# Layer 3 of a four-layer cross-attention kernel: the softmax probabilities transposed by VectorE and DMA in place of TensorE, with the work orders of layers 2 and 3 rewritten

## The reference, cut to what matters

```python
q = (hidden_state @ Wq + bq).reshape(b, l, KVH, GROUPS, HD).transpose(0, 2, 3, 1, 4)
k = (encoder_hidden_state @ Wk + bk).reshape(b, s, KVH, HD).transpose(0, 2, 1, 3)
v = (encoder_hidden_state @ Wv + bv).reshape(b, s, KVH, HD).transpose(0, 2, 1, 3)
scores = jnp.einsum('bkgld,bksd->bkgls', q, k) * scale + mask
attn = jax.nn.softmax(scores, axis=-1)
out = jnp.einsum('bkgls,bksd->bkgld', attn, v)          # needs the probabilities with s on partitions
x = out.transpose(0, 3, 1, 2, 4).reshape(b, l, H) @ Wo + bo + hidden_state
# layer norm of x, times gamma, plus beta
```

## Time and profile before

| what | value |
|---|---|
| median of three runs | 2391.65 us |
| the profiled execution itself | 2392.45 us |
| its span in the profile | 2390.7 us |
| TensorE matmul busy | 2244.4 us (94%) |
| VectorE, ScalarE, GpSimd busy | 1078.3, 1087.6, 580.0 us |
| mean granted clock of TensorE | 0.975 of full speed |

### The profile page before, as it was taken

How to read it: one execution, slowest core, us unless ns; L and a number is a source line. 1 busy time by engine, 2 the same in 40 slices (tenths; PEclk the granted TensorE clock), 3 DMA queues, 4 the chain that set the end, 5 groups by cost and what they waited for, 6 DMA issues and landing times. The chain is left out here.

```text
span 2390.7 us, 57498 instructions
## 1 busy us (share of the span) xinstructions
PE 2244.4 (94%) x22784; PEld 1637.0 (68%) x22784; DVE 1078.3 (45%) x3052; ACT 1087.6 (45%) x3441; POOL 580.0 (24%) x605
## 2 busy tenths in 40 slices
PE   7886999999999999999957999999999999999986
PEld 3444776676777777766546777777777777777754
DVE  4662322222222222222144565566665555666642
ACT  4553333333333333333223465566655655666554
POOL 0000100000000000000034444434444443344420
PEclk9997999999999999999978999999999999999998
DMA  4532000000000000000141001111010111110100
GB/s 163 171 105 64 16 19 19 19 19 19 19 19 19 19 19 19 19 10 5 76 133 21 16 21 26 22 26 22 21 26 16 26 26 22 26 21 16 21 20 10
DMA packets 116698, 81.94 MB, mean 34 GB/s; under 512 B 79136, under 2 KB 91808, under 8 KB 114208
## 3 DMA queue, kind: packets, MB, share of 16 engines
q1 hardware_dynamic: 106240, 48.35, 8.0%
...
...
## 5 line engine op out<-in xcount | busy, mean ns | idle before, releaser
L751 PEld LDWEIGHTS bank<-normedT,mlp_w 128*128 128x128 f32 x2048 | 235.0, 193 | 18.1 <-issue 17.1
L751 PE MATMUL bank<-normedT,mlp_w 128*128 128x128 f32 x2048 | 241.0, 278 | 0.8 <-DVE normedT L981 0.8
L761 PE MATMUL bank<-mlp_w,geluT 128*128 128x512 f32 x512 | 228.9, 596 | 0.0
L932 DVE CUSTOM_DVE_ANT_0 probs<-quad,neg_mask 128x256 f32<-128x256 f32 x256 | 90.8, 420 | 275.1 <-PE quad L681 275.1
L1975 ACT ACTIVATE scores<-scores,nmax 128x128 f32<-128x128 f32 x512 | 198.3, 396 | 2.5 <-DVE nmax L2237 2.5
L1463 POOL TENSOR_TENSOR k_even_odd<-k_even_odd,decay_products 128x512 f32<-128x512 f32 x80 | 98.1, 1227 | 328.1 <-PE quad L1659 251.6
L939 DVE COPY probsT<-quad 128x512 f32<-128x512 f32 x128 | 84.8, 683 | 191.6 <-PE quad L695 191.2
L761 PEld LDWEIGHTS bank<-mlp_w,geluT 128*128 128x128 f32 x512 | 93.8, 190 | 103.3 <-issue 103.3
L867 ACT ACTIVATE geluT<-bank,cols 128x128 f32<-128x128 f32 x256 | 73.0, 368 | 177.3 <-PE bank L751 177.3
L1391 POOL TENSOR_TENSOR gn_rstd<-gn_var_eps,halfs 128x32 f32<-128x32 f32 x16 | 87.0, 5435 | 170.2 <-DVE gn_var_eps L2160 170.2
L875 ACT ACTIVATE probs<-probs,nmax 128x256 f32<-128x256 f32 x256 | 126.1, 494 | 2.0 <-DVE nmax L932 1.8
...
## 6 DMA issues: line engine op xcount, KB each, us to landing
x_in<-in_x SPq DMA_DIRECT2D x32, 256.0 KB, 2.9
...
ctx_in<-in_ctx SPq DMA_DIRECT2D x16, 256.0 KB, 2.9
l_out<-wy ACTq DMA_DIRECT2D x16, 256.0 KB, 2.3
wy_in<-l_out SPq DMA_DIRECT2D x16, 256.0 KB, 3.5
hT<-in_ctxT SPq DMA_DIRECT2D x16, 256.0 KB, 3.5
l_out<-l_x ACTq DMA_DIRECT2D x16, 256.0 KB, 2.1
x_in<-l_out SPq DMA_DIRECT2D x16, 256.0 KB, 2.5
```

Source lines behind the costliest of these rows:

```text
L751: mm = nc.tensor.matmul(PS[b][:, f * P:(f + 1) * P], mlp_w1[:, c, m * P:(m + 1) * P], nT[:, c, :], start=(c == 0), stop=(c == NC - 1))
L761: mm = nc.tensor.matmul(PS[M.bank][:, :], gT[:, f, :], mlp_w2[:, f, :], start=(f == 0), stop=(f == NF - 1))
L932: mx = nc.vector.tensor_tensor_reduce(probs[:, h, :], PS[b][:, e * 256:(e + 1) * 256], negm[:, :], -1.0 / D1, 3.0e38, ALU.add, ALU.min, nm ...
```

## The change

The probabilities of all eight units now lie in one tile, `sc`, of nine rows of 512 numbers per partition. Row 0 is spare. The units of a half share four rows: unit k writes, for each of its four blocks of 128 columns, four runs of 32 numbers, one into each row of its half (`prob`). So a row holds 32-token blocks of every unit of its half. `a_turn` is now one VectorE instruction, which transposes each 32x32 block of row k+1 within its 32 partitions and writes row k. It can only start when the exponentials of the whole half are made. `a_move`, new on SyncE's queue, then moves four blocks of 32 partitions each to their place in `scT` with four transfers of 64 KB. `scT` is one tile for both halves, so `a_move` 4 to 7 wait until `a_value 0` is done. `a_value`, `a_norm` and `a_max` follow the new layout; VectorE's `a_norm` is two instructions. `v` now lies in the tile `z`, and `n_shift`, which writes `z`, waits for the spread of `v`. The PSUM copies of `a_turn` on ScalarE are gone. The banks and all five orders are new.

```diff
-        v = sb("v2", [P, NC, HC, D2])
+        v = z[:, :, :].rearrange("p c (h j) -> p c h j", h=HC)
...
-        sc = [sb(f"scores{u}", [P, 2, 2, P]) for u in range(NU)]
-        scT = [sb(f"probsT3_{q}", [P, 2, 2, P]) for q in range(RG)]
+        sc = sb("scores3_turned", [P, 2 * RG + 1, D])
+        scT = sb("probsT3", [P, 2, RG, D // 2])
...
         ORDER = dict(
-            pe=[("p_t5",), ("a_x",), ("w_var",), ("p_t5t",), ("b_out",), ("p_mix",), ("a_q",), ("a_kv",), ("p_mix4",), ("p_k",),
-                ("w_rstd",), ("a_score", 0), ("p_u1",), ("p_r",), ("a_score", 1), ("p_w",), ("w_out",), ("a_turn", 0), ("p_level",
-                0), ("p_g",), ("a_turn", 2), ("p_level", 1), ("w_xc",), ("p_v",), ("a_turn", 3), ("p_level", 2), ("a_turn", 1),
-                ("n_xa",), ("w_fr",), ("p_level", 3), ("w_fk",), ("p_level", 4), ("a_turn", 4), ("a_value", 0), ("a_turn", 7),
-                ("a_turn", 5), ("p_level", 5), ("a_turn", 6), ("w_fv",), ("p_level", 6), ("a_norm",), ("a_value", 1), ("p_s0",),
+            pe=[("p_t5",), ("a_kv",), ("p_t5t",), ("w_var",), ("a_x",), ("p_mix",), ("b_out",), ("a_q",), ("p_mix4",), ("p_k",),
+                ("w_rstd",), ("a_score", 0), ("p_u1",), ("p_r",), ("a_score", 1), ("p_w",), ("w_out",), ("p_level", 0), ("p_v",),
+                ("p_level", 1), ("w_xc",), ("p_g",), ("p_level", 2), ("w_fk",), ("p_level", 3), ("a_value", 0), ("n_xa",),
+                ("p_level", 4), ("w_fr",), ("p_level", 5), ("w_fv",), ("p_level", 6), ("a_norm",), ("p_s0",), ("a_value", 1),
                 ("p_av",), ("p_av6",)],
...
+            act=[("p_t5",), ("p_t5t",), ("a_kv",), ("a_x",), ("p_xm", 0), ("p_xm", 2), ("p_xm", 3), ("p_xm", 1), ("p_xm", 4),
+                 ("a_q",), ("p_k",), ("b_store",), ("p_u1",), ("w_rstd",), ("a_exp", 0), ("p_r",), ("p_w",), ("a_exp", 2), ("a_exp",
+                 3), ("a_exp", 1), ("a_exp", 7), ("a_exp", 6), ("p_v",), ("a_exp", 5), ("w_xc",), ("a_exp", 4), ("p_g",), ("w_fk",),
+                 ("n_xa",), ("w_fr",), ("a_norm",), ("p_level6",), ("a_bias",), ("p_wkv",)],
+            dve=[("n_ln1",), ("w_var",), ("p_xm", 0), ("p_xm", 2), ("n_nx",), ("b_out",), ("p_xm", 1), ("p_xm", 3), ("b_ln",),
+                 ("w_rstd",), ("a_max", 1), ("a_max", 0), ("a_max", 2), ("a_max", 3), ("p_xm", 4), ("w_gate",), ("a_max", 6),
+                 ("a_max", 5), ("a_max", 7), ("a_max", 4), ("p_rup", 0), ("w_out",), ("p_merge", 0), ("a_turn", 0), ("a_turn", 1),
+                 ("w_ln2",), ("a_turn", 2), ("p_merge", 1), ("a_turn", 3), ("p_rup", 1), ("w_sx",), ("w_xk",), ("p_s0c",), ("p_rup",
+                 2), ("p_merge", 2), ("w_xr",), ("a_turn", 4), ("a_rinv",), ("a_turn", 5), ("p_rup", 3), ("p_merge", 3), ("a_turn",
+                 6), ("p_gate",), ("a_turn", 7), ("p_rup", 4), ("p_merge", 4), ("p_merge", 5), ("p_rup", 5), ("n_shift",), ("p_rup",
+                 6), ("w_fv",), ("a_norm",)],
+            pool=[("n_rstd",), ("w_pow",), ("p_xm", 0), ("b_rstd",), ("p_xm", 2), ("w_first",), ("w_rep",), ("p_xm", 1), ("p_xm",
+                  3), ("p_k0",), ("p_ur",), ("p_wl",), ("w_rstd2",), ("p_kup", 0), ("p_xm", 4), ("p_kup", 1), ("p_kup", 2),
+                  ("p_kup", 3), ("p_kup", 4), ("p_s0b",), ("n_first",), ("a_x3b",), ("p_kup", 5), ("a_norm",)],
+            sp=[("a_move", 0), ("a_move", 1), ("p_v",), ("a_move", 2), ("a_move", 3), ("w_lda",), ("a_move", 4), ("a_move", 5),
+                ("a_move", 6), ("a_move", 7), ("n_ldx",), ("n_lds0",), ("p_ldw",)])
...
+        def prob(k, c, e):
+            at = 256 * e + 64 * (k % RG) + SB * c
+            return sc[:, RG * (k // RG) + 1:RG * (k // RG) + 1 + RG, at:at + SB]
...
+                def a_move(i, uses, k):
+                    half, m = k // RG, k % RG
+                    if half or later(i):
+                        sp.wait_ge(s_av, 2 * i + half)
+                    sp.wait_ge(s_turned, NU * i + k + 1)
+                    for q in range(RG):
+                        sp.dma_start(scT[SB * m:SB * m + SB, :, q, :],
+                                     sc[SB * q:SB * q + SB, k, :].rearrange("p (e n) -> p e n", e=2)).then_inc(s_moved, 16)
...
-                def a_turn(i, uses, k):
-                    pe.wait_ge(s_exp, NU * i + rank("act", "a_exp", k) + 1)
-                    turn4(uses[("a_turn", k)], BANK["a_turn", k], sc[k][:, :, :, :].rearrange("p a e q -> p (a e q)"))
...
-                    for t in latest([uses[("a_turn", RG * half + r)] for r in range(RG)]):
-                        pe.wait_ge(t.free, t.done)
+                    pe.wait_ge(s_moved, 16 * RG * (NU * i + RG * half + RG))
                     for e in range(2):
                         for r in range(RG):
                             mm = nc.tensor.matmul(PS[OAV][SB * r:SB * r + SB, half * 256:(half + 1) * 256], v3[:, r, e, :],
-                                                  scT[r][:, :, e, :], start=(e == 0), stop=(e == 1))
+                                                  scT[:, e, :, 64 * r:64 * r + 64], start=(e == 0), stop=(e == 1))
...
-                    nc.scalar.activation(scT[k % RG][:, :, :, :].rearrange("p a e q -> p (a e) q"),
-                                         chunked(PS[BANK["a_turn", k]][:, :]), ACT.Copy).then_inc(u.free, 1)
...
                 def a_norm(i, uses):
                     u, ps = use(uses, "a_norm")
+                    act.wait_ge(s_moved, 16 * RG * (NU * i + RG))
...
+                    if later(i):
+                        dve.wait_ge(s_v2, 64 * i)
                     nc.vector.tensor_tensor(sx[:, :, :], xaT[:, :, 0:P], xaT[:, :, 1:P + 1], ALU.subtract)\
...
+                def a_turn(i, uses, k):
+                    half = k // RG
+                    dve.wait_ge(s_exp, NU * i + 1 + max(rank("act", "a_exp", q) for q in range(RG * half, RG * half + RG)))
+                    if k == 0 and later(i):
+                        dve.wait_ge(s_attnT, i)
+                    elif k:
+                        dve.wait_ge(s_turned, NU * i + k)
+                    dve.sem_inc(s_hold, 1)
+                    nc.vector.transpose(sc[:, k, :], sc[:, k + 1, :]).then_inc(s_turned, 1)
```

More of the change, by code:

```diff
@@ L1157, in layers23 @@
         rinv = sb("rinv3", [P, KV3, G3])
[L1158 to L1160 removed]
+        attn = sc[:, 0, :].rearrange("p (c q) -> p c q", c=NC)
+        rrep, y, out = sc[:, 8, :], sc[:, 5, :], sc[:, 6, :]
         attnT = sb("attnT3", [P, NC, P])
@@ L1231, in layers23 @@
         S = {k: (sem(f"l23_{k}_psum_ready"), sem(f"l23_{k}_psum_free")) for k in ("quad", 5, 6, 7)}
-        USES = {("n_xa",): (7, 1), ("p_t5",): (6, 1), ("p_t5t",): (6, 1), ("p_mix",): ("quad", RG), ("p_mix4",): ("quad", 1),
-                ("p_u1",): (6, 1), ("p_w",): (6, 1), ("p_k",): (7, 1), ("p_r",): (5, 1), ("p_v",): (7, 1), ("p_g",): (6, 1),
+        USES = {("n_xa",): (5, 1), ("p_t5",): (6, 1), ("p_t5t",): (7, 1), ("p_mix",): ("quad", RG), ("p_mix4",): ("quad", 1),
+                ("p_u1",): (7, 1), ("p_w",): (7, 1), ("p_k",): (6, 1), ("p_r",): (5, 1), ("p_v",): (7, 1), ("p_g",): (7, 1),
@@ L1240, in layers23 @@
-                ("a_score", 1): ("quad", RG), ("a_turn", 0): (5, 1), ("a_turn", 1): (6, 1), ("a_turn", 2): (7, 1), ("a_turn", 3):
-                (6, 1), ("a_turn", 4): (5, 1), ("a_turn", 5): (7, 1), ("a_turn", 6): (5, 1), ("a_turn", 7): (6, 1), ("a_norm",): (5,
-                1), ("b_out",): (5, 1)}
+                ("w_var",): (6, 1), ("w_rstd",): (5, 1), ("w_out",): (6, 1), ("w_xc",): (6, 1), ("w_fk",): (6, 1), ("w_fr",): (6,
+                1), ("w_fv",): (5, 1), ("a_x",): (7, 1), ("a_q",): (7, 1), ("a_kv",): (5, 1), ("a_score", 0): ("quad", RG),
@@ L1252, in layers23 @@
[L1252 to L1262, removed]
@@ L1376, in after_first @@
                     sp.dma_start(W["Wo3"][:, :, :], a["Wo3"]).then_inc(s_w4, 16)
-                steps(sp, "sp", dict(after_first=after_first, n_lds0=n_lds0, n_ldx=n_ldx, p_ldw=p_ldw, w_lda=w_lda, p_v=p_v))
+                steps(sp, "sp", dict(after_first=after_first, n_lds0=n_lds0, n_ldx=n_ldx, p_ldw=p_ldw, w_lda=w_lda, p_v=p_v,
+                                     a_move=a_move))
             @block.gpsimd
@@ L1494, in a_norm @@
                 def a_norm(i, uses):
-                    u = uses[("a_turn", 1)]
-                    pool.wait_ge(u.ready, u.made)
+                    pool.wait_ge(s_turned, NU * (i + 1))
                     pool.wait_ge(s_rinv, i + 1)
@@ L1808, in _ @@
                                      w_rstd=w_rstd, w_out=w_out, w_xc=w_xc, w_fk=w_fk, w_fr=w_fr, w_fv=w_fv, a_x=a_x, a_q=a_q,
-                                     a_kv=a_kv, a_score=a_score, a_turn=a_turn, a_value=a_value, a_norm=a_norm, b_out=b_out))
+                                     a_kv=a_kv, a_score=a_score, a_value=a_value, a_norm=a_norm, b_out=b_out))
             @block.scalar
@@ L2003, in _ @@
                                        p_level6=p_level6, p_wkv=p_wkv, w_rstd=w_rstd, w_xc=w_xc, w_fk=w_fk, w_fr=w_fr,
```

(16 more changed lines are left out.)

30 lines of the change are left out of this document (13 added, 17 removed).

## The result

The changed kernel takes 2443.16 us (median of four runs, 2435.61 to 2445.85) against 2391.26 for the kernel before: ratio 1.021, 95% interval 1.019 to 1.0229. It is 52 us slower, where 45 us less was forecast, and lies outside the range.

A forecast was written before the change was run, and what follows sets the result against it. TensorE was taken to bound steps 3 to 16, busy 953.28 of 955.18 us. 14 x (4.1 - 0.6) = -49, steps 1 and 2 -2, steps 17 and 18 +6: -45 from 2392.45 gives 2347 us, range 2330 to 2384.

The forecast's parts named there:

- SyncE's moves: SyncE's queue: 32 transfers of 64 KB a batch, s = 0.43 us issue each (bounds 0.33 and 0.97), all hidden.
- rival C: SyncE's queue becomes the path: at s = 0.97 about 2515 us, slower from s = 0.73; chance 0.11, shared with VectorE late.
- 16s - 8.7: How late moves 0 to 3 land for the first half, in us a step, s being the issue time a transfer.
- 16s - 11.1: How late moves 4 to 7 land for `a_value 1`, in us a step, s being the issue time a transfer.
- The 4.1 us of turns: TensorE, each batch: eight groups of four transposes leave, at 0.52 us each, 4.1 us gained.
- net 3.5 a step: TensorE, steps 3 to 16: 4.1 us gained less a 0.6 us stall, 14 times, -49 us.
- rival A: VectorE's turn costs double, 1.4 us: 2388 us, no change; chance 0.04, shared with another way to nothing.
- rival D: Moves land in 4 us in place of 2: about 2365 us; chance 0.20, shared with a turn of about 1 us.
- Level 4's gap of half a us: TensorE ahead of level 4, each step: a stall of 0.5 to 0.6 us, waiting for VectorE's merge 3.
- Rival B: TensorE keeps all 4.1 us a step, level 4 starting without a stall: 2337 us; chance 0.10 for it and beyond.
- The tail: Steps 17 and 18 together: +6 us, step 18 baring the new chain of turns and moves.
- The head: Steps 1 and 2: about -1 us each, -2 (bounds -5, +4), as `n_shift` leaves the path between levels 3 and 5.

The follow-up runs named there:

- run through HBM: Changed kernel with each turned tile written to an HBM scratch and read back, 16 transfers a batch, spread of `v` behind read 3: 2365.68 us.
- filled wait: Changed kernel with 16 unread transposes of the identity added on TensorE ahead of `a_value 0`: 2411.39 us.
- idle alone: Kernel without moves, with `a_value 0` made to wait until VectorE has made turn 6: 2394.15 us.
- longer idle: Kernel without moves, with `a_value 0` made to wait for turn 7 in place of turn 6: 2437.56 us.
- kernel without moves: Changed kernel with the 32 transfers a batch left out, `a_value` reading zeros, the turns on VectorE kept: 2344.35 us.
- run with the spread moved: Changed kernel with only SyncE's order changed, the spread of `v` behind move 3 in place of move 1: 2392.48 us.

## Why the prediction was wrong

**The step that failed: SyncE's moves, "A move is nearer to the load in pieces; I take s = 0.43".** It measured 0.67 on average (median 0.60), and about as much with one piece a row (0.66) and on ScalarE's queue (0.76). The nearest row had been picked by the shape of the pieces. The runs point to where both ends lie: the loads and the store that were taken have HBM on one side, while the moves go from SBUF to SBUF. The cleanest pair is one turned tile of 256 KB in one transfer, 0.49 us at the median into SBUF and 0.34 into HBM. The run through HBM gains by both, the count and the price: 16 issues of 0.48 us on average in place of 32 of 0.67.

**A row with the same two ends was there.** The spread of `v` goes from SBUF to SBUF too, in transfers of 64 KB. The earlier trace rows has the second slowest of those in this stretch (3.88 us for four). All of them in the trace of before:

```profile
L1364 SPq DMA_DIRECT2D v_even_odd<-v x56: 602/678/1780, 1390.9 to 2273.4; - x56
```

Its median of 0.68 us is the moves' price to within 0.1 us, and the 0.97 was one slow step, not what short pieces cost. By rival C's formula 0.68 gives some 6 us less than before, 14 x (2.2 - 3.5) - 2 + 6 + 8, so the trace of before could have taken the gain from the forecast, but not foretold the loss.

**Rival C was right in kind, but its formula does not give the loss.** With s = 0.66, 16s - 8.7 makes the first half 1.9 us late (measured 2.7), 16s - 11.1 makes the second in time (it was: no wait at `a_value 1` in these steps). That would be 14 x (1.9 - 3.5) = -22, the head -2, and a tail of 6 + 32 x 0.23 = +13: some 11 us faster than before. C was said to make the kernel slower only from s = 0.73. It is slower at 0.66 because of a term that no part of the prediction had.

**The missing term: what an idle costs behind itself.** Every stall was priced at its length. In the trace of before TensorE had no stall of over 1.1 us in that stretch, so nothing there showed the price; it stood in the steps at the ends, where the earlier trace rows has the 64-matmul group of L1664 at 1.93 us behind a wait of 3.36, against 1.13 for the same group above in the changed kernel. The filled wait, the idle alone and the longer idle show that it exists and grows with the idle; it is 41.3 us of the 79.0 that the moves cost in the 14 steps, with the part above the straight line open as said.

**What held.** The 4.1 us of turns and the net 3.5 a step (955.18 - 907.74 = 47.4 against -49). The turn, 0.705 us against 0.72 with the wait, so rival A fell; the trace agrees with the estimate of 0.69 that was drawn from the Trainium skill (VectorE: DVE Perf Modes, The three transpose paths). The estimate of 0.43 us drawn from the 512 cycles of the Trainium skill (DMA: Bandwidth & Descriptors, Why a DMA increments its semaphore by 16 and not by 1) is met by the loads that stand behind another (0.43), lies above the first of a row (0.33) and below the moves (0.60 at the median); the measurement decides. Landing of 2.0 us held (median 2.0 in the run with the filled wait, which has the same moves), so rival D fell. Maxima and exponentials in their new shapes cost the same (0.29 and 0.39 us). Level 4's gap of half a us could not show in the changed kernel, since the wait ahead of `a_value 0` covered it; without moves it was 0.3. Rival B, 2337, was nearly reached by the kernel without moves (2344), but not by one that moves.

**The tail**, forecast at +6 for steps 17 and 18, was +22.2. Two bare halves of 16 transfers at about 0.6 us and 2.0 of landing are 11.7 us each, where 8.9 was laid out (5.6 of the 16.2); the comparison with the run without moves shows the rest. There steps 17 and 18 took 48.2 and 35.9 us, so all of the 22.2 comes with the moves: in step 17 waits for them of 0.81 and 4.32 us make 5.1 of 5.4, and in step 18 waits of 16.29 and 10.79 stand where 7.04 and 4.47 stood, 15.6 of 17.4. Some 2 us are left for the clock, which was low without moves too (0.82 and 0.71 against 0.84 and 0.63).

**The head**, -2 forecast, was -3.7.

**Still open.** In the run with the spread moved, TensorE waited up to 2.20 us ahead of `a_value 1`, and the matmuls behind it ran at full speed (1.07) every time; in the changed kernel, ahead of `a_value 0` a wait of 1.72 us had half speed behind it. The run with the spread moved also has one step with a gap of 0.60 us that nothing in the profile explains, right ahead of `w_fr`, and a slow `w_fr` behind it:

```profile
1781.84 0.20 PE L1677 MATMUL quad<-rT,k_even_odd 32*32 32x16 f32 x2 [0.60 <-issue]
1781.97 5.40 PE L1550 MATMUL bank<-Wfr,ffn_r_in 128*128 128x512 f32 x8
```

So length alone doesn't tell what an idle will cost; what TensorE did before differs (32-row matmuls of a level ahead of the costly ones, 128-row matmuls ahead of the cheap), and no run separates it from the rest. The filler is of the second kind as well, so the run with the filled wait doesn't say whether the shorter idle kept the clock or the work right ahead of it.
